# A six-layer decoder on one Trainium2 core: another merged order of the three instruction streams

## The reference

```
x = layernorm(x + nystrom_attention(x))         # 16 heads of 8, 64 landmarks, 6 Newton steps
x = layernorm(x + cross_attention(x, ctx))      # 16 heads of 8, linear relative bias
x = layernorm(x + top1_expert_ffn(x))           # 8 experts, hidden 256
x = layernorm(x + causal_attention(x))          # 16 heads of 8
x = layernorm(x + cross_attention_64(x, ctx, ctx, mask))   # layernormed q and k, 16 heads of 64
x = layernorm(x + gelu_ffn(x))                  # weights composed once from 32 low-rank factors
```

## Time and profile before

| | |
|---|---|
| median of 3 runs | 2513.37 us (2509.76 to 2516.99) |
| profiled execution, span | 2520.2 us |
| PE busy | 2266.3 us, 90% of the span |
| DVE busy | 1956.9 us, 78% |
| ACT busy | 1450.1 us, 58% |
| POOL busy | 387.1 us, 15% |
| mean granted TensorE clock | 0.953 |

### The profile page before, as it was taken

How to read it: one execution, slowest core, us unless ns; L and a number is a source line. 1 busy time by engine, 2 the same in 40 slices (tenths; PEclk the granted TensorE clock), 3 DMA queues, 4 the chain that set the end, 5 groups by cost and what they waited for, 6 DMA issues and landing times.

```text
span 2520.2 us, 95538 instructions
## 1 busy us (share of the span) xinstructions
PE 2266.3 (90%) x40576; PEld 1846.1 (73%) x40576; DVE 1956.9 (78%) x6166; ACT 1450.1 (58%) x5093; POOL 387.1 (15%) x530
## 2 busy tenths in 40 slices
PE   6789999999999999999999999999999999999875
PEld 3677777777777777777777777777777777777764
DVE  3568888888888888788888888788888888888652
ACT  3346666656656655656656565665656566566531
POOL 2101111111111111111111111111111111111110
PEclk9889999999999999999999999999999999999885
DMA  4200000000000000000000000000000000000000
GB/s 192 90 7 9 5 7 9 9 9 9 9 5 7 9 9 8 9 5 8 8 9 9 9 9 5 8 8 9 9 9 9 5 7 9 9 9 8 6 3 2
DMA packets 29960, 35.75 MB, mean 14 GB/s; under 512 B 3544, under 2 KB 28128, under 8 KB 28384
## 3 DMA queue, kind: packets, MB, share of 16 engines
q1 hardware_dynamic: 29536, 29.65, 3.4%
HBM read 27.54 MB, written 2.10 MB: 12 GB/s over the span
## 4 chain that ended last, share of the span: by engine, by line
PE 52%; DVE 28%; ACT 15%; issue 4%; POOL 0%; DMA 0%; SPq 0%; POOLq 0%; DVEq 0%; ACTq 0%
PE ps L477 29%; PE ps L480 8%; ACT probs L1062 5%; PE ps L744 4%; DVE probsT L1349 3%; PE ps L828 3%; ACT probs L1047 3%; PE ps L876 2%; ACT ey L985 2%; DVE x_rows L1211 2%; DVE small L1252 2%; PE ps L761 2%; PE ps L665 2%; DVE qk_v L1337 1%; DVE p L1254 1%
## 5 line engine op out<-in xcount | busy, mean ns | idle before, releaser
L1102 POOL TENSOR_TENSOR small<-small,weights 128x1 f32<-128x1 f32 x256 | 149.0, 582 | 1142.7 <-DVE small L1200 1142.7
L1010 ACT ACTIVATE probs<-ps,small 128x128 f32<-128x128 f32 x1024 | 286.1, 384 | 31.0 <-DVE small L1342 29.5
L1349 DVE COPY probsT<-ps 128x512 f32<-128x512 f32 x384 | 263.1, 685 | 36.3 <-PE ps L480 32.7
L480 PE MATMUL ps<-weights,probs 128*128 128x128 f32 x1536 | 256.1, 292 | 32.8 <-ACT probs L1010 15.4
L1342 DVE TENSOR_REDUCE small<-ps 128x4 f32<-128x512 f32 x384 | 254.2, 683 | 20.5 <-PE ps L828 10.7
L1113 POOL TENSOR_TENSOR probs<-probs,small 128x256 f32<-128x256 f32 x128 | 108.7, 849 | 885.6 <-DVE small L1478 885.6
L480 PEld LDWEIGHTS ps<-weights,probs 128*128 128x128 f32 x1536 | 178.7, 146 | 86.3 <-ACT probs L1010 44.6
L929 ACT COPY x_T<-ps 128x128 f32<-128x128 f32 x128 | 34.1, 267 | 302.9 <-PE ps L480 302.9
L1062 ACT ACTIVATE probs<-ps,small 128x128 f32<-128x128 f32 x512 | 181.6, 375 | 20.5 <-DVE small L1342 19.0
L477 PE MATMUL ps<-wz,ss 64*64 64x72 f32 x6144 | 157.4, 229 | 32.5 <-DVE wz L1294 32.4
L1293 DVE SCALAR_TENSOR_TENSOR wz<-ey,ss 128x256 f32<-128x256 f32 x320 | 142.0, 444 | 51.1 <-ACT ss L970 36.9
(11 more groups left out here) (199 smaller groups left out, 5400.0 us busy)
## 6 DMA issues: line engine op xcount, KB each, us to landing
weights<-in_wpack SPq DMA_DIRECT2D x3, 1759.0 KB
fc_A<-in_b SPq DMA_DIRECT2D x2, 2048.0 KB, 14.3
fc_A<-in_a SPq DMA_DIRECT2D x2, 2048.0 KB, 11.4
x_in_T<-in_xT SPq DMA_DIRECT2D x32, 64.0 KB, 1.8
x_in_rows<-in_x SPq DMA_DIRECT2D x32, 64.0 KB, 1.8
ctx_T<-in_ctxT SPq DMA_DIRECT2D x32, 64.0 KB, 1.9
ctx_rows<-in_ctx SPq DMA_DIRECT2D x32, 64.0 KB, 1.9
mask_i<-in_mask SPq DMA_DIRECT2D x32, 64.0 KB, 1.9
```

Of the source, the lines that this page charges most:

```text
L480: return nc.tensor.transpose(dst, src, ident)
L1010: ins = nc.scalar.activation(probs(s, g)[:, j], bank(s, SCORE_BANK[g], 128 * j, 128), ACT.Exp, bias=sm(s, "nb", 4 * g + j, 1), scale=-1.0)
L1102: nc.gpsimd.tensor_tensor(sm(s, out), sm(s, ve), w("mhalf"), ALU.pow).then_inc(sem(done, s), 1)
L1349: V.tensor_copy(probsT(s, n % 4).rearrange("p a b -> p (a b)"), bank(s, 2)).then_inc(sem("pT", s), 1)
```

## The change

The table `PLACES` is replaced by another of the same form; `PERIOD`, `START`, every step, buffer and wait stay. Cut to its core (the other lines of each engine change in the same manner):

```diff
--- before.py
+++ after.py
@@ -66,64 +66,64 @@
 PERIOD = 74.45336
 PLACES = {
     "sp": (
-        "n.xT 2.607  n.x 72.513  ",
-        "r1.ctxT 83.425  r1.ctx 83.485  rf.ln 233.799  ",
+        "n.xT 27.130  n.x 91.347  ",
+        "r1.ctxT 82.603  r1.ctx 86.108  rf.ln 312.566  ",
     ),
     "pe": (
-        "n.proj -6.362  n.v 6.575  n.a0 6.930  n.a1 9.337  n.a2 12.675  n.a3 15.620  n.b0 17.432  n.b1 17.846  "
-        "n.e3T0 20.498  n.e3T1 21.835  n.col0 24.435  n.col1 25.125  n.e1T0 26.271  n.e1T1 26.637  n.kk0 26.638  "
-        "n.kk1 27.564  n.y0 28.348  n.S0 30.103  n.W0 35.190  n.S1 36.219  n.W1 38.311  n.S2 40.807  "
-        "n.W2 46.082  n.S3 50.649  n.W3 57.265  n.S4 62.123  n.W4 63.130  n.S5 64.843  n.W5 66.411  n.w 67.483  "
-        "n.o 70.169  n.z 70.352  n.out 75.641  n.ln 80.473  ",
...
+        "n.proj -98.266  n.v 5.107  n.a0 12.836  n.a1 12.836  n.a2 14.157  n.a3 14.157  n.b0 17.385  "
+        "n.b1 17.559  n.e3T0 18.043  n.e3T1 25.454  n.col0 25.486  n.col1 26.473  n.e1T0 27.325  n.e1T1 27.325  "
+        "n.kk0 27.353  n.kk1 27.353  n.y0 27.938  n.S0 29.432  n.W0 33.966  n.S1 36.044  n.W1 38.377  "
+        "n.S2 43.103  n.W2 49.370  n.S3 53.276  n.W3 57.359  n.S4 61.329  n.W4 63.850  n.S5 66.065  "
+        "n.W5 67.324  n.w 68.426  n.o 71.242  n.z 73.908  n.out 77.259  n.ln 78.252  ",
+        "r1.proj 92.164  r1.s01 94.981  r1.t0 101.799  r1.t1 102.045  r1.v0 104.829  r1.v1 105.650  "
...
     ),
     "act": (
...
     ),
     "pool": (
-        "n.lm0 29.381  n.lm1 35.740  n.out 97.819  ",
-        "r1.ctx 135.356  r1.out 154.543  rm.out 170.775  r2.xbo 198.249  r2.out 198.282  ry.stats 204.577  "
-        "ry.xbo 209.993  ry.p0 223.550  ry.p1 225.077  ry.p2 231.021  ry.p3 241.150  ry.out 247.791  "
-        "rf.out 257.508  ",
+        "n.lm0 35.114  n.lm1 35.114  n.out 91.355  ",
+        "r1.ctx 131.670  r1.out 151.043  rm.out 163.438  r2.xbo 171.029  r2.out 205.117  ry.stats 205.117  "
+        "ry.xbo 208.079  ry.p0 208.888  ry.p1 210.385  ry.p2 230.330  ry.p3 230.590  ry.out 255.998  "
+        "rf.out 260.358  ",
     ),
     "dve": (
-        "n.lm0 2.692  n.lm1 4.279  n.v 4.799  n.a0 10.019  n.a1 12.416  n.a2 12.417  n.a3 12.789  n.p0 13.747  "
...
+        "n.lm0 3.391  n.lm1 3.573  n.v 5.516  n.a0 5.917  n.a1 6.673  n.a2 7.422  n.a3 8.440  n.p0 11.578  "
+        "n.b0 11.578  n.b1 11.578  n.p1 14.086  n.rd 20.751  n.E 24.595  n.y0 25.792  n.S00 27.229  "
...
+        "r1.q 87.537  r1.k 89.962  r1.v 90.072  r1.m0 91.921  r1.m1 93.111  r1.t0 97.633  r1.t1 101.476  "
+        "r1.ctx 101.476  r1.m2 103.286  r1.m3 103.875  r1.t2 112.405  r1.cn 112.812  r1.t3 113.002  "
...
     ),
 }
```

## The result

The changed kernel takes **3377.49 us** (median of 4 runs, 3373.22 to 3384.57) against 2515.18 us of the kernel before on the same chip (2509.76 to 2528.64): ratio **1.342, 95% interval [1.338, 1.347]**. The sign was as forecast, but the time lies 363 us above the forecast of 3014 us and outside the range.

A forecast was written before the change was run, and what follows sets the result against it. PE, 90% busy, was taken to bound the kernel: 68.5 work + 20.4 new + 2.3 old waits = 91.2 us per period, 90.4 taken; 2520.2 + 492 + 6 + 3 = 3021, less 6.8, gives 3014 us; range 2810 to 3120.

The forecast's parts named there:

- Fifteen new waits: PE steps that in the new order wait for a DVE or ACT producer; claimed sum 20.4 us per period.
- ry.xT: PE's transpose of x_norm, put ahead of n.S0 and r1.v0, waits for DVE's ry.norm: 2.4 us, the dearest.
- the small waits that stay: What remains of PE's old 5.5 us of idle per period after some 3.2 go: 2.3 us.
- the 90.4 taken: Forecast us per period, between 91.2 by sum and 89.8 step by step; 16.4 more than 73.96.
- The rival of soft waits: Waits partly counted twice, as a stall makes later inputs early: 8 to 12 us per period, about 2820 us; chance 0.14.
- faster: Rival: new order relieves DVE between n.proj and n.y0, PE sheds 2.1 us per period, 2448 us; chance 0.05.
- nothing changes: Rival: the places differ but the order on PE hardly does; chance 0.03.
- The waits before r1.z, n.W0 and n.W5: Old PE waits claimed to go, part of some 3.2 us per period; the one before r1.z is 0.85.
- SP's order of transfers in the steady stretch stays: Premise that, with instructions and waits unchanged, only each PE step's wait for its DVE or ACT producer needs costing.
- should take the 0.34: DVE's rf.ln, 0.95 us beside POOL's n.lm1, to fall to 0.34; the 0.6 us saved not on PE's path.
- the clock case: Rival: granted clock falls from 0.97, or more waits of the kind come; over 3080 us, chance 0.12.
- The sign that the forecast gave for the clock's part: PE busy clearly over 2350 us at a clock of 0.85 or less.

The follow-up runs named there:

- a_ctx_ahead: Changed kernel with SP loading ctx_T for a lane's next batch ahead of the store of its last output; 3172.65 us, ratio 1.259.
- a_q_fill: Changed kernel with r1.proj's q products ahead of the ctx_T wait and made four times over, 24 of them useless per batch; 3283.42 us, ratio 1.303.
- a_q_first: Changed kernel with r1.proj's first 8 products (q) taken out from behind the wait for ctx_T; 3470.24 us, ratio 1.377.
- a_xT_fill: Changed kernel with 16 transposes of the identity put into PE's pause before ry.xT; 3294.09 us, ratio 1.307.
- a_two_back: a_rfln_early with PE's ry.xT also put back, behind r1.v1 instead of ahead of n.S0; 3075.33 us, ratio 1.220.
- b_xT_early: Kernel before with r.ln3 and ry.xT on PE ahead of r1.v0 and ry.norm on DVE behind r1.ctx; 2660.79 us, ratio 1.056.
- a_rfln_early: Changed kernel with DVE's rf.ln put back right behind n.a3 instead of behind n.b1; 3273.62 us, ratio 1.300.
- b_rfln_late: Kernel before with only DVE's rf.ln moved behind n.b1; 2642.85 us, ratio 1.049.
- a_ctx_fill: Changed kernel with both the edit of a_ctx_ahead and the filler of a_xT_fill; 3105.37 us, ratio 1.233.
- b_ctx_ahead: Kernel before with SP loading ctx_T for the lane's next batch ahead of the store of its last output; 2518.12 us, ratio 0.999.

## Why the prediction was right and wrong

**Right: the mechanism and the waits that it named.** Fifteen new waits were summed; all fifteen are there:

| | forecast | measured | | forecast | measured |
|---|---|---|---|---|---|
| r2.t1 | 1.5 | 1.51 | r1.s23 | 0.8 | 0.70 |
| n.a2 | 1.1 | 1.14 | n.S1 | 1.0 | 1.08 |
| n.a3 | 1.3 | 1.17 | r1.t3 | 1.15 | 1.01 |
| r2.t3 | 0.9 | 0.88 | r.ln1 | 1.65 | 1.45 |
| r1.s01 | 1.7 | 1.74 | rm.gT | 0.5 | 0.30 |
| n.col0 | 1.5 | 1.20 | ry.s23 | 1.85 | 1.79 |
| r.ln3 | 1.4 | 1.13 | n.S5 | 1.65 | 1.67 |
| ry.xT | 2.4 | 2.27 | sum | 20.4 | 19.04 |

With the small waits that stay (0.15 to 0.81, 2.42 in all against 2.3; the one before n.S2 grew from 0.45 to 0.81) that is 21.5 us of idle time against the 21.9 in the 90.4 taken. The rival of soft waits falls with it, and so do the rivals "faster" and "nothing changes". The waits before r1.z, n.W0 and n.W5 went, as said.

**Wrong, first step: "SP's order of transfers in the steady stretch stays, so only this is to be costed."** The order stays, the times don't. For each PE step I looked for what it waits for on DVE and ACT, but not on the queue of SP. The load of ctx_T has two waits ahead of it, its own and that of the store, and the second hangs on a DVE step that the change moves. The forecast even named this step: rf.ln "should take the 0.34", and its 0.6 us "aren't on PE's path in the new order". It costed the step's duration and not its place. Worth: 4.2 us per period as idle time; a_ctx_ahead gives back 6.8 with its share of the clock.

**Wrong, second step: "The point forecast takes nothing" for the clock.** The range reaches "past the clock case", which was an estimate of mine: 3 us per period, 3105 us in all. No run shows that term. What the runs showed in its place is a clock of 0.88 in the steady stretch and 8.1 us per period (76.72 against 68.64). The time at half clock is 23.9 us of 102.4, and PE is at work in most of it, in 20.7 of the 23.9 us: behind the pauses lies a block of products with no wait in it, which takes up to 1.8 times as long (2.05 against 1.13 us for the 8 products over x_firstT). Reckoned per us of added half clock, the work grew by 8.1 / 20.0 = 0.40. The row that should have told it was the earlier trace rows, 0.61 against 1.06 us for the same piece of r2.proj. The sign that the forecast gave for the clock's part half came: PE is busy for 2518.1 us, clearly over 2350, but at a clock of 0.873, not at 0.85 or less.

More work for PE at the same place lowered the time at half clock: the useless products of a_q_fill take it from 36.5 to 17.7 us per period, and the total is 187 us under that of a_q_first.

That a pause brings a stretch at half clock is shown at ry.xT, by filling the pause, by taking it away and by putting it in (at half clock per period: a_xT_fill 11.95 us against 23.89, a_two_back 9.56 against 23.89, b_xT_early 10.75 against 3.92). At r1.proj it is shown only for the changed kernel as a whole: a_rfln_early and b_rfln_late took away and put in 3.4 to 3.6 us of pause, and the half clock mostly moved to or from another place (23.89 us in all as before, and 4.61 against 3.92). What decides where the clock falls stays open.

**By how much each.** Of the 12.0 us per period that were missing, 4.2 are SP's queue and 8.2 the clock (76.72 against the 68.5 of the forecast), less 0.4 of waits summed too high (21.9 against 21.5). The two are not independent: some of the 8.2 is behind the 4.12-us pause. a_ctx_fill is the nearest to the forecast's own terms, without SP's wait and without the pause at ry.xT: 93.4 us per period and 3105 us, its 10.6 us at half clock still in it, against 90.4 and 3014.

**What was not tried.** To exchange the whole table of one engine alone would have told how the loss divides over PE, DVE and ACT. The orders of the engines must fit together, and whether such a mixture runs at all was not tried either, so this stays open.

## What to carry to other kernels

When steps are reordered, follow for every PE step not only the engine that it waits for but each queue in between: a load that stands in a queue behind a store inherits the store's wait, and then a DVE step that nobody on PE needs sets PE's start (4.12 us of wait in the changed kernel, 3.56 in b_rfln_late). Issue such loads as soon as their buffer is free, ahead of any wait of another kind; here it cost nothing (b_ctx_ahead, ratio 0.999), and with it the late rf.ln made no wait at r1.proj (a_ctx_ahead). In this kernel of small float32 products a pause of 2.00 us cost 4.5, with 6.8 us more at half clock behind it (b_xT_early), while 3.4 to 3.6 us of pause elsewhere cost about their length. Take both as bounds of a pause's price, and read it from the granted clock of short stretches, not from the mean.
